# A mixture-of-experts and attention kernel: the weights sent by SyncE behind x, a longer ring of places, another order

## The reference, cut to what matters

```python
x = x + 0.5 * ffn(layernorm(x), gate_w, w1, w2, w3)
x = x + attn(layernorm(x), W_q, W_k, gain, bias, log_mix, log_scale)
x = x + 0.5 * ffn(layernorm(x), gate_w, w1, w2, w3)
# ffn:
weights, idx = top_k(softmax(x @ gate_w.T), 2);  weights /= weights.sum()
out_e = (silu(x @ w1[e].T) * (x @ w3[e].T)) @ w2[e].T      # 512 wide, 8 experts
result = sum over the 2 chosen experts of weights * out_e
# attn:
sim = x @ x.T / 16, strictly causal; keep the 8 largest of each row
attn = softmax(q @ k.T / sqrt(32)) over those;  msg = attn @ x
delta = gelu((mix * x + (1 - mix) * msg) * gain + bias) * scale
```

## Time and profile before

| | |
|---|---|
| median of 3 runs | 896.85 us (896.12 to 900.83) |
| the profiled execution | 894.73 us, of which its span is 893.0 |
| PE, DVE, ACT, POOL busy | 80%, 63%, 57%, 43% of the span |
| mean granted TensorE clock | 0.935 |
| DMA | 147.76 MB, mean 165 GB/s |

### The profile page before, as it was taken

How to read it: one execution, slowest core, us unless ns; L and a number is a source line. 1 busy time by engine, 2 the same in 40 slices (tenths; PEclk the granted TensorE clock), 3 DMA queues, 4 the chain that set the end, 5 groups by cost and what they waited for, 6 DMA issues and landing times. The chain is left out here.

```text
span 893.0 us, 17410 instructions
## 1 busy us (share of the span) xinstructions
PE 716.3 (80%) x4672; PEld 432.9 (48%) x4672; DVE 559.7 (63%) x1596; ACT 512.6 (57%) x954; POOL 379.8 (43%) x433
## 2 busy tenths in 40 slices
PE   1652425799989998889998798889998889997971
PEld 1551213446645555554555455555554445654641
DVE  6728881233367786786879787888684514335753
ACT  4727831263357896866889688865874323332320
POOL 4447874213322325465365634564364522221211
PEclk9975588899999999999999999999999989999986
DMA  6953237466796878797987877797878677678995
GB/s 239 429 196 93 93 102 169 108 110 140 132 212 116 127 157 135 144 194 158 178 170 181 166 163 145 138 185 150 153 137 166 150 169 142 128 134 234 218 279 178
DMA packets 328213, 147.76 MB, mean 165 GB/s; under 512 B 309501, under 2 KB 312445, under 8 KB 327357
## 3 DMA queue, kind: packets, MB, share of 16 engines
q1 hardware_dynamic: 314301, 97.61, 57.2%
q0 software_dynamic: 13824, 49.04, 16.8%
HBM read 33.96 MB, written 43.14 MB: 86 GB/s over the span
## 5 line engine op out<-in xcount | busy, mean ns | idle before, releaser
L1161 PE MATMUL B<-t_W,t_ht 128*128 x1704 | 406.1, 388 | 49.5 <-DMA t_ht<-hs 38.6
L939 POOL DMA_INDIRECT yt<-t_W,t_idx x142 | 148.8, 1048 | 388.6 <-ACT t_W L1305 338.4
L1161 PEld LDWEIGHTS B<-t_W,t_ht 128*128 128x128 f16 x1704 | 167.4, 99 | 233.7 <-issue 75.8
L1654 DVE SCALAR_TENSOR_TENSOR t_th<-B,t_K,t_th 128x512 f32<-128x512 f32 x142 | 105.9, 748 | 134.5 <-PE B L1161 93.3
L1173 PE MATMUL B<-t_W,t_gh 128*128 x1140 | 142.8, 276 | 24.7 <-DMA t_gh<-t_gp 18.4
L1289 ACT ACTIVATE t_th<-B,t_K 128x512 f32<-128x512 f32 x142 | 96.8, 683 | 106.7 <-PE B L1161 89.1
L1173 PEld LDWEIGHTS B<-t_W,t_gh 128*128 128x128 f16 x1140 | 109.3, 99 | 61.0 <-issue 37.0
L921 POOL DMA_INDIRECT hs<-t_s,t_POS x112 | 117.1, 1045 | 47.7 <-issue 25.5
L1305 ACT ACTIVATE t_W<-B 128x256 f32<-128x256 f32 x142 | 53.1, 374 | 98.1 <-PE B L1173 87.4
L1660 DVE TENSOR_TENSOR t_gp<-t_th,t_gp 128x512 f16<-128x512 f32 x95 | 66.9, 707 | 32.6 <-ACT t_gp L1298 29.0
L1298 ACT ACTIVATE t_gp<-t_th 128x512 f16<-128x512 f32 x95 | 58.8, 624 | 42.1 <-DVE t_th L1654 28.1
(11 more groups left out here) (205 smaller groups left out, 855.3 us busy)
## 6 DMA issues: line engine op xcount, KB each, us to landing
t_W<-wk POOLq DMA_DIRECT2D x6, 2048.0 KB, 13.3
t_hp<-yt SPq DMA_DIRECT2D x16, 512.0 KB, 4.4
t_s<-yt SPq DMA_DIRECT2D x15, 512.0 KB
t_X<-x SPq DMA_DIRECT2D x8, 512.0 KB, 7.3
out<-t_X SPq DMA_DIRECT2D x7, 512.0 KB, 5.8
hs<-t_ph SPq DMA_DIRECT2D x18, 136.0 KB
t_ht<-hs SPq DMA_TRANSPOSE x142
t_idx<-hs SPq DMA_DIRECT2D x142, 0.5 KB
```

The lines of the kernel that those rows point to most:

```text
L939: eng.indirect_dma_start(yt_d[L], bass.IndirectOffsetOnAxis(ap=IDX[:, n % RING:n % RING + 1], axis=0), YO[n % 3], None).then_inc(d_y[n % 3 ...
L1161: t = eng.matmul(B[b][:], HT[n % 3][:, (2 * hl + db) * 128:(2 * hl + db) * 128 + 128], W16[:, bass.ds(expert[n] * 4096 + (db * 2048 + wl * ...
L1654: eng.scalar_tensor_tensor(out=th[:], in0=B[b1][:], scalar=K[:, 7:8], in1=th[:], op0=ALU.mult, op1=ALU.mult).then_inc(free[b1], 1)
```

## The change

Three edits. The six weight transfers leave GpSimd and are issued by SyncE after x, the log factors and the bias, with no wait. RING grows from 8 to 16, so that a load needs the put 16 tiles back and no longer the one 8 back. And ORDER is another string; it has the same 2908 steps. The buffer counts of HT, YO, TH and the gate products get names (HTR, YR, THR, LAG) with the values that they had.

```diff
-RING = 8
+RING = 16
...
 LAG = 3
+HTR = 3
+YR = 3
+THR = 2
 PS = 1
...
 ORDER = (
-    "z())Bt%))B))t%feBtYYfe))YBYtKLKL$$KLKL$$%)%)Bqxw+++tf1feYeYpYKLKLvD%Y!!!!!!$))Bt$KLKL-+f+$++!+++++!>es)YY$KL++++"
...
+    "))Bt)%)Bztf%e))fYYeBK)(YYLKL$$tKLKL)$)B$%t)B++q%xfteYYf+weYKLKLpv!!!!!!!!Y)))%)$$KLDK-Lfe+++++++$$+++++++++++B1Y"
...
-            yield tile("load", (n,), after + ((("up", (n - 3, 1)),) if n >= 3 else ()) +
+            yield tile("load", (n,), after + ((("up", (n - HTR, 1)),) if n >= HTR else ()) +
                        ((("put", (n - RING,)),) if n >= RING else ()))
...
@@ gpsimd, "root" @@
                     eng.tensor_tensor(ve[:, 1, :], ve[:, 0, :], mhalf[:], ALU.pow).then_inc(s_rstd, 1)
-                    if n == 2:
-                        e.wait_ge(d_x[5], 16)
-                        for i in range(6):
-                            eng.dma_start(W[:, 4 * i + 2:4 * i + 6, :],
-                                          wk_d[:, 4 * i:4 * i + 4, :]).then_inc(d_w[i], 16)
...
@@ sync @@
             eng.dma_start(bias[:], bias_d).then_inc(d_bias, 16)
+            for i in range(6):
+                eng.dma_start(W[:, 4 * i + 2:4 * i + 6, :], wk_d[:, 4 * i:4 * i + 4, :]).then_inc(d_w[i], 16)
...
@@ sync, "load" @@
                     if n >= RING:
-                        e.wait_ge(d_y[(n - RING) % 3], 16 * ((n - RING) // 3 + 1))
+                        e.wait_ge(d_y[(n - RING) % YR], 16 * ((n - RING) // YR + 1))
```

More of the change, by code:

```diff
@@ new lines @@
+    "Pr>;;$$>WQt%WSqF***.fPx;;N.We>E;;>wQQYpYTNSFSPTuEFs1.v;DE*;P)N)BW.SPNQWum>Q!t%Ff-onm&one;.Y/;ENY>;;>#QW::F&<SSPZ"
+    "/;&W.G<NEijP!***$;##FE>.!/ZQlSV;<;$WGiZPQNj>d&*qxlF#E;GSbCP/.;biFNjS.!A*<Nb>ZWEQQw;;d*PSF*PCGlijpEAF.ubW>dCN;WE."
+    ";FSld>;;>*A*PCWuN.Nv;QAWQQ;WuOWESP.!r!FSN>;;E>;FPQS))B.t%NPEf**!FQWQeY;>;SPYWE.N.SFP;::>;;.NN>EF;;SP$$sWqxw.QQ>E"
+    ";;WNpv**FESSDP!QWu-[FQ**W!EF.E>;;>hhh*NSPP!QE.;;>NFF.;Q***WSPNSP;>EWhhhE.NSPW;;>;.N;FQVQF>W.;SsP.hhQN;>EESF;;h!P"
+    "NS.N>**!QFuWWEE;;>;QWWSP.P;NFS.QNQP>E*uWQF;.**FS;>N;PS.P**EF*EF*Ws;>NS;W;QuQP.y1>EF*;W.NSP;W>;;.QNSN>EEFQ;;EFE>S"
@@ L505, in tanhs @@
         for n in range(N):
-            yield tile("tanh", (n,), (("up", (n, 0)),) + ((("glow", (n - 2,)),) if n >= 2 else ()),
+            yield tile("tanh", (n,), (("up", (n, 0)),) + ((("glow", (n - THR,)),) if n >= THR else ()),
                        gives=(("x", n, 0),))
@@ L526, in evicts @@
         for n in range(N):
-            yield tile("evict", (n,), (("down", (n,)),) + ((("put", (n - 3,)),) if n >= 3 else ()),
+            yield tile("evict", (n,), (("down", (n,)),) + ((("put", (n - YR,)),) if n >= YR else ()),
                        gives=(("y", n),))
@@ L651, in macaron_kernel @@
         AT = [sb(f"at{i}", [128, 16], F32) for i in range(4)]
-        HT = [sb(f"ht{i}", [128, 512], F16) for i in range(3)]
-        TH = [sb(f"th{i}", [128, 512], F32) for i in range(2)]
+        HT = [sb(f"ht{i}", [128, 512], F16) for i in range(HTR)]
+        TH = [sb(f"th{i}", [128, 512], F32) for i in range(THR)]
         wqs = [P16[:, 256 + 128 * i:384 + 128 * i].rearrange("p (a b) -> p a b", a=2) for i in range(2)]
@@ L667, in macaron_kernel @@
         d_gw, d_qk, d_lg, d_gain, d_bias = (sem(n) for n in ("d_gw", "d_qk", "d_lg", "d_gain", "d_bias"))
-        d_in = [sem(f"d_in{i}") for i in range(3)]
-        d_y = [sem(f"d_y{i}") for i in range(3)]
+        d_in = [sem(f"d_in{i}") for i in range(HTR)]
+        d_y = [sem(f"d_y{i}") for i in range(YR)]
         d_sc = [[sem(f"d_sc{i}{h}") for h in range(2)] for i in range(5)]
@@ L675, in macaron_kernel @@
         d_ph = [sem(f"d_ph{i}") for i in range(2)]
-        d_gt = [sem(f"d_gt{i}") for i in range(3)]
+        d_gt = [sem(f"d_gt{i}") for i in range(LAG)]
         d_g = [[sem(f"d_g{i}{h}") for h in range(2)] for i in range(6)]
@@ L814, in stored @@
         def stored(n):
-            return [16 * ((n - i) // 3 + 1) for i in range(3)]
+            return [16 * ((n - i) // YR + 1) for i in range(YR)]
         def joined(L, tile):
@@ L1286, in _ @@
                     e.wait_ge(s_kk, N_K1)
-                    if n >= 2:
-                        e.wait_ge(s_gl, n - 1)
-                    eng.activation(TH[n % 2][:], B[b][:], ACT.Silu, scale=K[:, 0:1]).then_inc(free[b], 1)
+                    if n >= THR:
+                        e.wait_ge(s_gl, n - THR + 1)
+                    eng.activation(TH[n % THR][:], B[b][:], ACT.Silu, scale=K[:, 0:1]).then_inc(free[b], 1)
                 elif kind == "high":
```

93 lines of the change are left out of this document (44 added, 49 removed).

## The result

| | before | after | ratio, 95% interval |
|---|---|---|---|
| median | 898.84 us of 4 (896.12 to 902.61) | 874.34 us of 4 (873.50 to 875.79) | 0.973 (0.968 to 0.977) |
| once more | 896.72 us of 11 (893.81 to 902.09) | 877.56 us of 6 (871.55 to 883.76) | 0.978 (0.974 to 0.983) |
| profiled execution, its span | 894.73, 893.0 | 874.94, 873.0 | |

What follows compares the result with a forecast made beforehand. VectorE was taken to set the pace until 130 us, TensorE from 200 us on. Savings of 5.2 + 2.0 + 1.5 = 8.7 us from 894.73 gave 886.0, or 888 us as median of the runs; range 879 to 900.

Steps and rivals of the forecast that it cites:

- (1): Front: weights issued by SyncE follow x without the 4.3 us gap and end at 45.1 us, 53.3 at worst.
- (2): Front: scatters get their own ring and advance beside the weights; first scatter about 30.3 us, eight issues end at 40.4.
- T: Front: time when the first scatters have landed and GpSimd goes on; 53.90 us before, 45 forecast.
- rival A: Front: scatters aren't held up at all, GpSimd goes on at 41 us, kernel takes 884 us; chance 0.22.
- (3): Front: both power operations behind all four scatter pairs lose 5.7 us at equal T; VectorE resumes at 57.2, 3.2 gained.
- (4): Front, after VectorE resumes: its idle time shrinks by 2.0 us of 0 to 4; last piece split 5.2 us earlier.
- (5): Ramp, 136 to 200 us: loads 6, 7 and 8 ahead of most pads save 2.0 us of 0 to 5.
- (6): RING 16, mainly the last stage, 680 to 862 us: earlier loads cut TensorE's waits, 1.5 us of 0 to 6.
- (7): Middle, 200 to 680 us: effect of the new order taken as 0, bounds 9.4 us either way.
- Rival B: Middle, 200 to 680 us: takes the front's gain back, TensorE idles 9.4 us more, 897 us; chance 0.21.
- Rival C: Front: weights move at x's 330 GB/s and are served first, T 54.3, kernel takes 903 us; chance 0.13.

Runs made afterwards that it cites:

- w_only: Kernel before with only the six weight transfers moved from GpSimd to SyncE, old order and RING 8: 880.75 us, ratio 0.985 to before; timed again 883.68 us, 0.988.
- order_only: Kernel after with the six weight transfers given back to GpSimd, new order and RING 16 kept: 881.74 us, ratio 0.990 to the kernel before.
- cut_front: Kernel after with the new order only up to step 261, the first transpose of a gate product, then the old relative order: 885.31 us, 0.994 to before.
- cut_ramp: Kernel after with the new order only up to step 440, tile 11's gate-product transpose, then the old relative order: 880.17 us, ratio 0.987 to before.
- old_front: Kernel after with the old relative order up to step 264, the first transpose of a gate product, then the new one: 873.85 us, 0.975 to before.
- ring8: Kernel after with RING 8, loads that this forbids standing behind their put: 917.15 us, ratio 1.022 to the kernel before.
- after_again: The kernel after, unchanged, timed once more: 877.56 us, ratio 0.978 to the kernel before.
- roots: Kernel after with group 5's power operation on GpSimd behind two pairs of second scatters instead of four: 875.77 us, ratio 0.978 to the kernel before.

## Why the prediction was wrong

- **(1) Weights on SyncE: right.** They are issued from 7.25 in 4.69 us, and 426 GB/s followed, against 421 taken. The last wait of TensorE for them ends at 48.61 and not at 45: scattered rows move beside them (0.69 MB from 16 to 45 us, beside 11.62 MB on SyncE's queue), and from 45 to 50 GpSimd's queue moved 0.98 MB and SyncE's 0.26. The Trainium skill (DMA: Bandwidth & Descriptors, Specifications) gives a core about 358 GB/s, a stack's rate divided over two cores; the 426 of this core over 29 us lie above that share.
- **(2) Scatters beside the weights: the direction right, T too late.** First scatter 30.68 (30.3 said), the eight end at 41.03 (40.4 said). The first COPY follows with no wait, so T is 41.04: rival A's 41, not my 45. TensorE still waited for weights until 48.61, so those rows landed beside them. In place of the wait before T there are 2.4 us in two waits behind it.
- **(3) What the order takes back: right in kind, and the time met by luck.** At equal T a loss of 5.7 was worked out. Without the new order VectorE resumes at T + 6.5 (w_only), with it at T + 12.9 (order_only, 12.2 said): 6.4. In the kernel after it is T + 15.3, the 12.9 and the 2.4 us of the two waits. VectorE resumed at 56.30 (57.2 said), but by two errors that nearly cancel: T came 4.0 us earlier than I had it, and the way from T took 3.1 longer.
- **(4) VectorE's idle time: sized small.** 66.6 us from there to the last split, 3.1 less than before where 2.0 was taken. The last piece was split 7.2 us earlier, 5.2 said; at gate 3 6.1 of that are left.
- **(5) The ramp: the step that failed.** 2.0 of 0 to 5 was taken, and 10.0 came (13.6 in order_only); TensorE's idle time in 136 to 200 fell by 7.0 of 14.4. I had read the right stretch and the wrong thing in it. I named the load of tile 6 at 148.04 and then discounted it; moved by itself, with those of tiles 7 and 8, it costs 2.5. That the order of the ramp's steps makes the gain is shown (order_only, cut_front against cut_ramp, old_front). How is shown in part. The old order had a ring of waits over four engines: product of tile 3, its transpose, the load, the last scatter behind the puts. Three of the lists, changed together, take 6.7 us of it away; alone GpSimd's gives 3.4, and the others cost 6.5 and 15.2. What the remaining 3 to 7 us are is open. The trace of before had two signs, SyncE's wait for a scatter in 145 to 175 us, and the last scatter behind the put of tile 4; I read neither:

```profile
SPq L62 <- DMA hs<-t_s,t_POS: 2.9, 1, 2.9
```
```profile
166.31 0.95 POOL L939 DMA_INDIRECT yt<-t_W,t_idx  x1 [4.39 <-ACT t_W L1305]
...
169.23 1.11 POOL L921 DMA_INDIRECT hs<-t_s,t_POS  x1 [0.30 <-issue]
```

- **(6), (7) Ring, late and middle: the sign right, the size small.** 1.5 and 0 were taken, and 4.4 came behind gate 20 (6.6 in the second execution): 6.0 behind gate 80, less 1.6 between gates 20 and 80. The ring's wait itself, 1.8 us on SyncE before, gave nothing that the times can tell (1.000, within 0.3%). What the ring is for is the order: ring8 loses 36 us without it.
- Rival B, that the middle gives the gain back, did not come: TensorE is idle 1.2 us more there. Rival C, weights at x's rate, neither.

The sum was 5.2 + 2.0 + 1.5; what was measured is 6.1 + 10.0 + 4.4 - 0.5 = 20.0. Terms (5) and (6) were bounded by the waits of single instructions, each taken by itself, and with 10.0 where 5 was the most allowed for the ramp even the range's end was too short.

## What to carry to other kernels

When a new order moves steps on several engines at once, don't price each move only by the wait in front of it: follow the ring of waits once round (here load, product, eviction, put, scatter, load), and take TensorE's idle time of the stretch as the upper bound, not a part of it. Changing one engine's list of such a ring can cost more than the whole ring gives. And a gain can hide a loss: the weights' move alone gave 10.7 us at the front, of which the new order took 4.6 back, and only the two halves run apart showed that.

## What the runs showed of the hardware

TensorE late at the front. In after_again 11.8 us of waits in 36 to 60 us are put down to nothing that the profile shows, in nine waits of up to 1.9 us before the scoring products and six of up to 0.9 before the sums; in the profiled execution of the same program for the first comparison there were none. Of the 20 profiled executions four show 7.7 to 13.3 us of it, those of after_again, roots, ring8 and old_front. The DMA carried the same in both executions of the kernel after: 36 to 54 us in after_again, then in after:

```profile
36.00:54.00 18.00, 6.24 (x59) 4.19 (x56) 2.74 (x19) 1.10 (x4) 13.54 (x18) 0.69 0.76 306
```
```profile
36.00:54.00 18.00, 9.55 (x149) 9.03 (x146) 2.90 (x20) 2.06 (x5) 12.14 (x16) 0.91 0.75 302
```

59 products against 149, at the same 0.76 and 0.75 of DMA share. The mean granted clock in the late execution is 0.69; after TensorE has stood among these waits it is granted 0.50, the 1.2 GHz level, from 44 to 56 us:

```profile
44.00:56.00 12.00, 5.56 (x44) 3.98 (x45) 0.45 (x2) 0.00 (x0) 8.39 (x11) 0.50 0.46 175
```

What holds TensorE's instructions back there is open; the kernel before shows 4.4 us of it in the same place, so it isn't the change's doing.
